# Scales folded into weights, inputs rounded two pairs ahead, and expert rows scatter-added in DRAM: one change to a two-layer kernel

## The reference

```python
logits = ht @ gate_w
top_vals, top_idx = jax.lax.top_k(logits, K)            # K = 2
gates = jax.nn.softmax(top_vals, axis=-1)
for e in range(E):                                       # E = 8
    we = jnp.sum(gates * (top_idx == e), axis=-1)
    ye = jax.nn.silu(ht @ w1[e]) * (ht @ w3[e]) @ w2[e]
    out = out + we[:, None] * ye
return out + residual
...
def _reorder_quantize_x(x, idx):
    scale = jnp.max(jnp.abs(x)) / GLOBAL_DIV
    xr = (x / scale)[:, idx]
    scale_x = jnp.max(jnp.abs(xr), axis=1, keepdims=True) / FP8_MAX
    qx = _fp8(xr / scale_x)
    return (qx, scale_x, scale)
...
qx, sx, sc = _reorder_quantize_x(xf, up_reorder_index)
g = _qlinear(qx, sx, sc, w_gate, up_reorder_index, out_idx=down_reorder_index)
u = _qlinear(qx, sx, sc, w_up, up_reorder_index, out_idx=down_reorder_index)
t = jax.nn.silu(g) * u
qt, st, sct = _reorder_quantize_x(t, down_reorder_index)
y = _qlinear(qt, st, sct, w_down, down_reorder_index)
```

## Time and profile before

| | before |
|---|---|
| device time, median of 3 runs (lowest to highest) | 705.23 us (705.21 to 707.87) |
| the profiled execution's own time | 705.76 us |
| its span | 703.9 us |
| PE busy | 503.7 us (72%) |
| DVE busy | 539.9 us (77%) |
| ACT busy | 342.4 us (49%) |
| POOL busy | 287.7 us (41%) |
| mean granted clock of TensorE | 0.883 |

### The profile page before, as it was taken

The page is one execution under the profiler, slowest core; times in us unless marked ns, Lnnn a source line. Parts: engine busy times, 40 slices in busy tenths (PEclk is TensorE's granted clock), DMA queues, the critical chain, the costliest instruction groups (busy, mean ns, idle before and its releaser), DMA issues.

```text
span 703.9 us, 9187 instructions
## 1 busy us (share of the span) xinstructions
PE 503.7 (72%) x2954; PEld 342.0 (49%) x2954; DVE 539.9 (77%) x1004; ACT 342.4 (49%) x737; POOL 287.7 (41%) x232
## 2 busy tenths in 40 slices
PE   2011385799999999983589899999899980363442
PEld 1001132578888788863256566666566650132221
DVE  4999685788888889844288698787976853799983
ACT  3235154677777787830244645456255531342231
POOL 3454035644444455223534855332520004664250
PEclk9999999899999999995699999999999995555555
DMA  9200011400000000009216531604251002010000
GB/s 264 92 0 0 0 55 65 155 4 1 1 1 1 1 17 17 1 31 312 73 31 213 172 46 61 194 27 171 38 180 65 15 16 68 16 52 8 16 16 15
DMA packets 28314, 44.23 MB, mean 63 GB/s; under 512 B 4779, under 2 KB 21419, under 8 KB 28011
## 3 DMA queue, kind: packets, MB, share of 16 engines
q1 hardware_dynamic: 20843, 31.43, 13.8%
q0 software_dynamic: 3024, 8.14, 4.8%
q10 hardware_dynamic: 4400, 4.06, 1.7%
HBM read 38.51 MB, written 5.12 MB: 62 GB/s over the span
## 4 chain that ended last, share of the span: by engine, by line
PE 47%; DVE 30%; issue 10%; ACT 6%; POOL 5%; DMA 1%; SPq 0%; ACTq 0%; DVEq 0%; POOLq 0%
PE pb L405 9%; PE pw L405 9%; PE pb L581 6%; PE sc L444 6%; PE sc L581 5%; PE po L405 4%; PE pt L455 3%; DVE areg L1045 2%; DVE areg L1031 2%; DVE areg L1029 1%; PE pt L590 1%; POOL breg L1583 1%; DVE areg L1042 1%; DVE areg L1286 1%; DVE areg L1378 1%
## 5 line engine op out<-in xcount | busy, mean ns | idle before, releaser
L581 PE MATMUL pb<-wreg,areg 128*128 x184 | 84.8, 604 | 1.1 <-ACT areg L892 0.8
L1555 POOL TENSOR_TENSOR breg<-breg,con 128x512 f32<-128x512 f32 x32 | 40.7, 1270 | 82.9 <-ACT breg L794 82.9
L405 PE MATMUL pb<-areg,wreg 128*128 128x512 f16 x240 | 60.8, 391 | 14.8 <-ACT breg L794 9.4
L405 PE MATMUL pw<-areg 128*128 128x256 f16 x406 | 59.5, 283 | 8.7 <-DVE areg L1386 8.7
L581 PE MATMUL sc<-wreg,areg 128*128 x184 | 63.2, 486 | 0.0
L802 ACT ACTIVATE breg<-breg,mx 128x128 f32<-128x128 f32 (+1 forms) x128 | 56.6, 445 | 1.9 <-DVE mx L1153 1.7
L1597 POOL DMA_INDIRECT areg<-h_dram,row_ids x23 | 32.1, 1396 | 57.9 <-PE po L573 39.9
L581 PEld LDWEIGHTS pb<-wreg,areg 128*128 128x128 f32 x184 | 33.9, 195 | 36.5 <-issue 36.2
L405 PEld LDWEIGHTS pw<-areg 128*128 128x128 f16 x406 | 40.7, 101 | 19.3 <-DVE areg L1386 12.2
L444 PE MATMUL sc<-areg,breg 128*128 128x128 f32 (+1 forms) x256 | 49.5, 338 | 0.4 <-DVE mx L1153 0.4
L1550 POOL TENSOR_TENSOR breg<-breg 128x512 f32<-128x512 f32 x32 | 44.5, 1392 | 4.5
(11 more groups left out here) (237 smaller groups left out, 1336.2 us busy)
## 6 DMA issues: line engine op xcount, KB each, us to landing
wreg<-in_L_ffn_w SPq DMA_DIRECT2D x24, 896.0 KB
ys_dram<-areg ACTq DMA_DIRECT2D x23, 128.0 KB
wreg<-in_L_ffn_wq SPq DMA_DIRECT2D x1, 2048.0 KB, 9.6
wreg<-in_L_ffn_wo SPq DMA_DIRECT2D x1, 2048.0 KB, 8.1
areg<-in_fside_BxSxS ACTq DMA_DIRECT2D x4, 256.0 KB, 5.9
x_in<-in_x SPq DMA_DIRECT2D x4, 256.0 KB, 4.1
h_dram<-areg SPq DMA_DIRECT2D x8, 128.0 KB, 1.9
out_dram<-areg SPq DMA_DIRECT2D x8, 128.0 KB, 1.7
```

What stands on the lines that cost most here:

```text
L405: last = nc.tensor.matmul(bank, w(a), m(b), start=first and k == 0, stop=final and k == 2)
L581: last = nc.tensor.matmul(bank, xsT[:, parity, c * P:(c + 1) * P], wreg[:, bass.ds(base + (m * C + c) * FF + lo, w)], start=c == 0, stop=c ...
L1555: G.tensor_tensor(t2[:, parity, :].rearrange("p (b n) -> p b n", b=2), t2[:, parity, :].rearrange("p (b n) -> p b n", b=2), rope_sin.rearr ...
```

## The change

Five things change together; line numbers below are those of the changed kernel.

1. **Expert rows.** The router also sorts the gates by slot (`hot_gate`, 16 more matmuls, `slot_gate`), so that ACT's copy of the down product already carries the gate. POOL then adds each tile's 128 rows into token rows of `x1_dram` by an indirect DMA with an add (`add_rows`), one at a time, each behind the landing of the one before, since two tiles can hold the same token. `x1_dram` is written first from `x0` by SP, 9 transfers. After the last add SP loads `x1` back, 4 transfers. The gathers, the combine and ACT's 23 stores go.
2. **POOL's order.** `x0 + x_in` moves from tiles 18 to 21 to a place behind the first four gathers, and `add_rows(n - 6)` stands behind `gather_tiles(n)`.
3. **Folded scales.** POOL multiplies the rounded gate and up weights by their column scales (`fold_scales`), ACT and DVE split the product into high and low f16 halves (`fold_high`, `fold_low`), and the gate and up product takes 16 matmuls a tile in place of 8. ACT makes Silu straight from PSUM; the column scaling, ACT's sigmoid and copy, and both products on POOL go.
4. **Rounding.** ACT makes two scaled copies, one of them larger by 2**20, and DVE rounds with three instructions in place of four. ACT also scales the input.
5. **Order of the quantised part.** The first two pairs are rounded before the first gate product, the others two pairs ahead; ACT takes all sigmoids first; POOL only adds the input.

```diff
+            def add_rows(n):
+                pool.wait_ge(s["y_copied"], n + 1)
+                if n == 0:
+                    pool.wait_ge(s["add_ids_ready"], 1)
+                    pool.wait_ge(s["x1_init"], 16 * (NT + 1))
+                else:
+                    pool.wait_ge(s_y[(n - 1) % 2], 16 * ((n - 1) // 2 + 1))
+                G.indirect_dma_start(out=x1_dram[:, :], out_offset=bass.IndirectOffsetOnAxis(ap=add_ids[:, n:n + 1], axis=0),
+                                     in_=ysb[:, n % 2, :], in_offset=None, compute_op=ALU.add).then_inc(s_y[n % 2], 16)
...
-                    act.wait_ge(s_y[1 - parity], 16 * ((n + 1) // 2))
-                    nc.scalar.activation(ysb[:, 1 - parity, :], pw[:, 0:D], ACT.Copy, scale=1.0 / WS).then_inc(s["y_copied"], 1)
-                    act.wait_ge(s["y_copied"], n)
-                    act.dma_start(ys_dram[(n - 1) * P:n * P, :], ysb[:, 1 - parity, :]).then_inc(s_y[1 - parity], 16)
+                    if n >= 3:
+                        act.wait_ge(s_y[1 - parity], 16 * ((n - 1) // 2))
+                    nc.scalar.activation(ysb[:, 1 - parity, :], pw[:, 0:D], ACT.Copy, scale=slot_gate[:, n - 1:n])\
+                        .then_inc(s["y_copied"], 1)
+                if n in (20, 21):
+                    fold_high(n - 20)
...
+            for k in range(2):
+                sp.wait_ge(s_y[k], 16 * ((MT + 1 - k) // 2))
+            for p in range(NT // 2):
+                sp.dma_start(x1[:, 2 * p:2 * p + 2, :], x1_dram[2 * p * P:(2 * p + 2) * P, :].rearrange("(i p) d -> p i d", p=P))\
+                    .then_inc(s_x[p], 16)
...
+            for n in range(MT):
+                gather_tiles(n)
+                if n >= 6:
+                    add_rows(n - 6)
+                if n == 3:
+                    add_conditioned()
+                    recurrence_inputs(1, 0)
...
+            def fold_low(m):
+                dve.wait_ge(s["fold_high"], m + 1)
+                V.scalar_tensor_tensor(w_fold[m][:, 1], fold[m], WS, w_fold[m][:, 0], ALU.mult, ALU.subtract).then_inc(s["fold_low"], 1)
...
+                if n >= MT - 2:
+                    fold_low(n - MT + 2)
...
+                        for c in range(C):
+                            for a in range(2):
+                                last = nc.tensor.matmul(bank, qxT[:, c, :], w_fold[m][:, a, c, k * IH:(k + 1) * IH],
+                                                        start=c == 0 and a == 0, stop=c == C - 1 and a == 1)
...
             for i in range(NT):
-                if i + 1 < NT:
-                    gate_of_tile(i + 1)
-                act.wait_ge(s["inv_ready"], i + 1)
-                nc.scalar.activation(tscaled, tval, ACT.Copy, scale=rs[:, 8, i:i + 1]).then_inc(s["scaled_ready"], 1)
...
+                scaled_inner(i)
+                if i % 2 == 0 and i + 4 < NT:
+                    scaled_input((i + 4) // 2)
                 if i + 2 < NT:
                     copy_qxT(i + 2)
+                    gate_of_tile(i + 2)
```

345 lines of the change are left out of this document (195 added, 150 removed).

## The result

The changed kernel takes 689.02 us (median of 4 runs, 685.10 to 689.36) against 706.55 for the kernel before on the same chip (4 runs, 705.21 to 710.05): a ratio of 0.973, 95% interval 0.968 to 0.978. It is faster, inside the range, and 9 us slower than the 680 of the forecast. Its profiled execution took 689.36 us, with a span of 687.5.

What follows compares the result with a forecast made beforehand. PE was taken to bound the loop, DVE and hand-offs the quantised part. Loop +7.0 put the last copy's end at 588.1, x at 594.3; plus 78, 6.0 and 1.9 gave 680.2, less 0.5 for the median: 680, range 668 to 697.

Steps and rivals of the forecast that it cites:

- First tile +5.2: Loop's first Silu: four additions on POOL ahead of batch 0's inputs delay it by 5.2 us (4.8 to 5.8).
- Second add +1.3: Loop, tile 5: the second add on POOL stands ahead of batch 1's inputs, for which ACT waits; 1.3 us later.
- Third add +1.2: Loop: ACT's copy of tile 4's product waits for the third add to land; the next Silu starts 1.2 us late.
- X: Time of an indirect add from start of issue to landing; taken as 3.5 us, at least 2.9, up to 6 in range.
- Chain of adds 3 to 5: Loop, ahead of batch 2's inputs: adds chained X apart end about 430, ACT wants them about 436; covered to X about 5.4.
- x additions moved, -1.2: Loop, tiles 14 and 15: additions of x no longer run beside DVE's w2 split; 1.2 us given back (0 to 2).
- Later adds: Rest of the loop: adds keep pace, one a tile of 9.3 us; they cost nothing, up to 1 us.
- `fold_low` +0.5: Behind the last tile: DVE's second `fold_low` pushes the low half of the last product by 0.5 us (0 to 1).
- Hand-over 6.2: Between loop and quantised part: x is there 6.2 us after the last copy's end, in place of 11.0 to the sigmoid.
- Rival (a): Quantised part: PE's clock stays low, a tile takes 9.5 us, 92 in place of 78; 694 us, chance 0.13.
- rival (b): Loop: slow adds; X of 6 to 8 gives 685 to 693 (chance 0.07), X of 10 gives 711 (beyond 705: 0.06).
- Rival (d): Quantised part: DVE's and ACT's order makes waits of 1.5 us more a tile; 692 us, chance 0.10.

Runs made afterwards that it cites:

- four_products: The changed kernel with four buffers for the down products in place of two, so ACT's copy waits for the add four tiles back; 687.30 us.
- fold_only: The changed kernel with products stored by tile, gathered and combined as before, so only the quantised part is changed; 686.38 us.
- scatter_only: The changed kernel with the quantised part of the kernel before, so products are still added into token rows in DRAM; 710.28 us.

## Why the prediction was right or wrong

- **Direction and share of the gain: right.** The quantised part gave the gain. Forecast from x's landing to the last output 78; measured 601.32 to 680.86 (680.38 and 0.48), 79.5. First output forecast +31, measured +31.5 (632.78); the seven others 45 and 2 for dips, measured 47.6.
- **First tile +5.2: right in this place.** Measured 5.07. It was taken for POOL's time ahead of batch 0's inputs alone, and that was its mechanism. The same four additions cost about 4.5 and 5 us in two other places, where POOL idled, by holding DVE.
- **Second add +1.3: 1.27 at tile 5, right by luck.** POOL's time for an add was taken as a gather's, 0.94 and 0.30; it was 3.25 here and 2.18 on average. But batch 1's inputs behind it took 3.95 us in place of 6.25 (before: 391.29 to 397.54), which gave 2.3 us back. The add's landing held ACT just as long by another way: the copy that waited for it at 404.22 and a table load put ACT's exponentials at 406.03, when the inputs had ended at 406.00. Another 0.55 had come by tile 2: the up product behind PE's wait of 4.80 us took 6.08 us, at a granted clock of 0.50 to 0.85. In four_products it took 5.39, and this 0.55 is missing.
- **Third add +1.2: 4.7. The term that was mis-sized most.** The step: "lands X later ... With X = 3.5". Its X was 7, over the 6 that the prediction itself named as a sign of being wrong; the median of all 23 was 4.4. The step priced the add by gathers with nothing beside them, and did not count the send of scales that the same queue had just taken. With the send moved, X was 4.3, the add was issued 1.6 us earlier, and this term came to 0.8.
- **Chain of adds 3 to 5 covered: right, but by luck.** They stood 4.6 us apart, and were covered only because ACT was late already. Four buffers took that delay away, and ACT waited 5.05 us for the inputs behind the chain.
- **x additions moved, -1.2: -3.75.** One row of 3.17 against 2.02 was taken for the whole. Beside the additions a `TENSOR_SCALAR` of 128x512 on DVE had also taken 1.37 us in place of 0.43, which makes 2.1 of PE's wait, and the product behind the wait ran at the lower clock, 1.7 more. The prediction had no term for what a wait of PE does to its clock inside the loop.
- **Later adds "nothing, up to 1": 0.65 up to tile 14.** Another 1.4 came at tile 20, and it is not the adds' alone. DVE's w2 split ran there beside POOL's second product of folded weights (545.63 for 3.44):

```profile
545.46 5.50 DVE L1452 SCALAR_TENSOR_TENSOR areg<-wreg,areg 128x1792 f16<-128x1792 f16 x1 [0.27 <-issue]
```

  The same split takes 3.55 us in fold_only, where no add stands between the two products, and 2.02 in scatter_only, which makes no such product; both lose nothing at this tile. So an add and a product on POOL together cost it. The prediction counted these products only for what they do to the adds, not for what they do to DVE.
- **`fold_low` +0.5: 1.75** from the last Silu to the last copy (13.96 against 12.21) in this trace. The low half of the product comes 0.2 us later than before (9.32 behind the Silu against 9.12), and 0.55 later than in scatter_only; the rest is the last product at the lower clock, 3.80 us against 2.46, which is not the edit's: it is missing in six of the twelve traces with it.
- Sum of the loop from the ids on: 5.07 + 0.55 + 1.27 + 4.74 - 3.75 + 2.04 + 1.75 = 11.7 in place of 7.0, just beyond the 4 to 11 given.
- **Hand-over 6.2 from the copy's end to x: 6.9** (7.35 from its start): the last add was issued 0.75 behind the copy's start, SP's loads followed 3.83 later, and x took 2.8 where 2.6 was taken.
- **The quantised part: right in size.** The working took 12.5 us for a tile before, which is 100 us over eight tiles; between outputs it was 10.3. No term hangs on it.
- **The clock: half right.** High from the first or second tile on, with some dips, was the assumption, and over 0.8 its sign; the granted clock was 0.72 on average, 0.84 at best in the stretches above, and the late gaps between outputs were 5.9 to 7.6 us, the last 4.2. Rival (a), clock stays low, did not come.
- Of the 9.2 us between 680.2 and 689.36, the loop holds 4.7, the part ahead of the ids 1.6 (which this change doesn't touch), the quantised part 1.5, the hand-over 0.7, and the end of the span 0.6 (6.6 behind the last output in place of 6.0).
- The time fell where rival (b) had X of 6 to 8 (685 to 693), but (b) came only in part: X was 4.4 in the median and near 7 or more for six of the 23 adds, and the late third add makes 3.5 of the 9.2 us. Rival (d) at 692 did not come: the quantised part took 1.5 us more in all, not 1.5 a tile. That the time lies inside the range is in part luck, since terms missed by -2.6, +3.5, +2.0 and +1.3 us partly cancel.

## What to carry to other kernels

Replacing a gather and combine behind a loop by scatter-adds inside it takes 1.5 to 3.9 us of POOL a tile and builds a serial chain of 4.4 us a tile or more. Here it cost 12.4 us and gave back 11.1, and 5 of the 12.4 were not the adds but the four additions that had to stand ahead of them; so the parts of a change should be tried apart, and each placed apart. When a transfer is put into a queue, look at what that queue took just before: a send of 704 elements of 4 bytes made the next add land 2.7 us later. An engine that idles is not a free place for work if another engine is held by it: moving four additions into idle time of POOL cost DVE, and PE behind it, nearly as much as leaving them. And a short wait of PE can cost more than itself: behind waits of 2.6 to 4.9 us the same product of 21 matmuls took up to 4.13 us in place of 2.47.

## What the runs showed of the hardware

- Four elementwise instructions of POOL in a row (4.9 us) held one small DVE instruction (cast of 128x16, `TENSOR_SCALAR` of 88x8) until the last of them ended: 4.43 and 3.35 us in place of 0.17. A maximum over 2048 columns and a reciprocal beside them were not slowed. A larger DVE instruction (the w2 split, 128x1792) took 3.17 us beside one addition and 5.50 beside a product of 1408 columns, in place of 2.02. Beside POOL's making of descriptors for four accumulating DMAs (5.07 us) the same `TENSOR_SCALAR` took 0.17 us.
- An indirect add of 128 rows of 1 KB into DRAM, in the changed kernel: 1.54 us at least and 2.18 on average on POOL, landing 3.7 us at least, 4.4 in the median, 9.4 at most. Of the six that took about 7 us or more, two stand right behind a send of scales and three beside an expert's weights (324 to 358 GB/s); the sixth (552.14, 7.3 us) stands by neither. Only the send was tried. Without the addition 0.97 and 1.64 us on POOL. "DMA: Bandwidth & Descriptors" of the Trainium skill (anatomy of one DMA) fits 2.3 us for its bytes, an estimate; no add here came near that.
- The granted clock fell behind some waits of PE in the loop (0.59 behind one of 2.62 us before), but not behind each: behind the wait of 2.8 us ahead of the last product, six of twelve traces have the product at 2.46 us and six at 3.80 to 4.12 (granted clock 0.65 over that stretch in the changed kernel).
- Why POOL needs 3.25 us for one add and 1.6 for the next was not tried. It stays open.
- The time up to the router differs by 5 us between executions of kernels that do the same there.
